# Attention's weighing products in blocks of two pieces, and the sign matrices copied to scratch in the read stage instead of stored by attention

## The reference, cut to what matters

```python
x = x + tanh(g_xattn) * layer(layernorm(x), pos, ...)     # layer: read, attention, write, read, mlp, write
x = x + tanh(g_ffn) * (layernorm(x) @ sign) * softplus(scale)

def attention(qkv_in, qkv_w, pos):        # 2 batches, 16 heads of 32, 1024 positions, causal
    q, k, v = projections; q, k = rope(q, pos), rope(k, pos)
    scores = where(tril, q k^T / sqrt(32), -1e30)
    p = softmax(scores); return p v
```

## Time and profile before

| | |
|---|---|
| median of 3 runs (range) | 2181.62 us (2178.24 to 2190.67) |
| profiled execution, its own time | 2191.2 us |
| its span, first to last instruction | 2189.2 us |
| read, attention and block stage in it | 365.3, 451.9 and 1372.0 us |
| busy in the span: PE, DVE, ACT, POOL | 90%, 61%, 40%, 22% |
| moved by transfers | 464.72 MB, mean 212 GB/s |

### The profile page before, as it was taken

How to read it: one execution, slowest core, us unless ns; L and a number is a source line. 1 busy time by engine, 2 the same in 40 slices (tenths; PEclk the granted TensorE clock), 3 DMA queues, 4 the chain that set the end, 5 groups by cost and what they waited for, 6 DMA issues and landing times.

```text
span 2189.2 us, 25299 instructions
## 1 busy us (share of the span) xinstructions
PE 1968.7 (90%) x9818; PEld 1345.7 (61%) x9818; DVE 1327.3 (61%) x1403; ACT 881.2 (40%) x1191; POOL 478.8 (22%) x362
## 2 busy tenths in 40 slices
PE   4789988999999994399989999999999999989997
PEld 0344456555555552178677777777777677666776
DVE  5476667546666638858468549558458567567100
ACT  4646653546666654162362430162530261432000
POOL 0022342786665630000000001000001100011010
PEclk8889997879999996699999999999999999999999
DMA  7548358999999814337467658677658677668676
GB/s 261 158 111 226 116 152 190 310 275 265 288 278 278 243 64 172 151 135 293 145 270 273 230 163 236 201 264 281 226 151 232 192 284 276 242 156 238 158 175 132
DMA packets 156283, 464.72 MB, mean 212 GB/s; under 512 B 34176, under 2 KB 34816, under 8 KB 138752
## 3 DMA queue, kind: packets, MB, share of 16 engines
q1 hardware_dynamic: 123568, 324.16, 47.6%
q0 software_dynamic: 30432, 128.46, 19.1%
q10 hardware_dynamic: 2160, 10.43, 1.3%
HBM read 323.79 MB, written 139.20 MB: 211 GB/s over the span
## 4 chain that ended last, share of the span: by engine, by line
PE 42%; DVE 7%; DMA 7%; ACT 4%; issue 2%; SPq 0%; POOL 0%; DVEq 0%; POOLq 0%; ACTq 0%
PE ps L1833 15%; PE ps L1643 8%; PE ps L1645 7%; PE ps L1644 7%; DMA sign_h<-sign_h_scratch 5%; DMA up<-up_s_scratch 2%; PE ps L1702 1%; PE ps L1711 1%; ACT L1862 1%; DVE Y L2156 1%; PE ps L1663 1%; PE ps L1752 1%; PE ps L1740 1%; DVE DL_attn L2063 0%; DVE E_attn L2068 0%
## 5 line engine op out<-in xcount | busy, mean ns | idle before, releaser
L1833 PE MATMUL ps<-XH,sign_h 128*128 128x512 f32 x768 | 310.2, 404 | 18.5 <-DMA sign_h<-sign_h_scratch 14.1
L1833 PE MATMUL ps<-XL,sign_h 128*128 128x512 f32 x768 | 303.6, 395 | 0.0
L1209 DVE TENSOR_REDUCE maxes<-ps 128x1 f32<-128x512 f32 (+3 forms) x384 | 208.0, 555 | 156.1 <-PE ps L1059 117.6
L1155 ACT ACTIVATE probs<-ps 128x512 f32<-128x512 f32 (+3 forms) x384 | 169.0, 489 | 133.5 <-PE ps L1086 86.5
L1643 PE MATMUL ps<-ZH,up 128*128 128x512 f32 x512 | 204.4, 399 | 13.6 <-DVE ZL L2181 8.9
L1645 PE MATMUL ps<-ZH,up 128*128 128x512 f32 x512 | 200.5, 392 | 0.0
L1644 PE MATMUL ps<-ZL,up 128*128 128x512 f32 x512 | 200.3, 391 | 0.0
L1833 PEld LDWEIGHTS ps<-XH,sign_h 128*128 128x128 f32 x768 | 146.6, 191 | 67.8 <-DMA sign_h<-sign_h_scratch 18.1
L1101 PE MATMUL ps<-probs,values 128*32 128x512 f32 (+3 forms) x768 | 170.0, 519 | 0.1
L1101 PE MATMUL ps<-probs,ones_sum 128*32 128x512 f32 (+3 forms) x768 | 170.0, 519 | 0.0
L1833 PEld LDWEIGHTS ps<-XL,sign_h 128*128 128x128 f32 x768 | 146.7, 191 | 31.9 <-issue 1.9
(11 more groups left out here) (337 smaller groups left out, 4156.5 us busy)
## 6 DMA issues: line engine op xcount, KB each, us to landing
sign_h<-sign_h_scratch SPq DMA_DIRECT2D x256, 256.0 KB, 4.3
up<-up_s_scratch SPq DMA_DIRECT2D x58, 1024.0 KB, 6.3
proj<-proj_s_scratch SPq DMA_DIRECT2D x58, 640.0 KB, 4.0
X<-in_x_read POOLq DMA_DIRECT2D x16, 1024.0 KB, 9.0
xn_scratch<-X SPq DMA_DIRECT2D x16, 1024.0 KB, 14.1
sign_raw<-in_sign SPq DMA_DIRECT2D x32, 512.0 KB, 10.2
sign_h_scratch<-sign_high SPq DMA_DIRECT2D x32, 512.0 KB, 8.1
up_s_scratch<-weight_split SPq DMA_DIRECT2D x16, 1024.0 KB, 8.7
```

Of the source, the lines that this page charges most:

```text
L1155: eng.activation(PT[p % NPT][:, e, 0:w], ps[:, score_bank(v, p, e), 0:w], ACT.Exp, scale=HD ** -0.5).then_inc(ex.sem, ex.unit)
L1209: eng.tensor_reduce(MAXES[:, e, q, k0 // T:k0 // T + 1], ps[:, ring_bank(n, ("max", m)), 0:w], AX.X, ALU.max).then_inc(mx_read.sem, mx_rea ...
L1833: mm = eng.matmul(ps[:, sign_bank(m)], s[q][:, f], x[:, n], start=n + w == 0, stop=n == NF - 1 and w == len(operands) - 1, skip_group_chec ...
```

## The change

Three edits.

1. `weigh` runs in blocks of two pieces. Round n handles its pieces in six groups of two: all scores and maxima of the two pieces, then `rows` if due, then the weighing of the two pieces before. The last two pieces of a pair are weighed at the start of the next round. In a piece, each of the two scores is now followed by its part of the maxima. There is a fourth buffer of probabilities.
2. Attention no longer stores the high halves of the signs. POOL still computes both halves, for the test whether a low half is needed.
3. The scratch that the last stage loads is filled by 16 transfers of 1 MB from the input tensor straight to the scratch tensor, in SP's queue of the read stage, four in each of the passes n = 1..4. (In the branch with low halves, the last stage would cut the signs itself.)

```diff
 read_phase, SP
+                def copy_sign(m):
+                    eng.dma_start(io["sign_s"][m], io["sign"][m]).then_inc(t["sign_copied"].sem, t["sign_copied"].unit)
                 for n in range(NB + 1):
+                    if n:
+                        copy_sign(4 * n - 4)
                     for tt in range(TT if n else 0):
                         store_v(n - 1, tt)
...
+                    if n:
+                        copy_sign(4 * n - 3)
                     for s in (1, 2):
                         for u in range(TT if n else 0):
                             store_qk(n - 1, s, u)
+                        if n:
+                            copy_sign(4 * n - 3 + s)
                     if 0 < n < NB:
                         load_turns(n)
 attention_phase
-        NPT = 3
+        NPT = 4
 SP
                 def store_weights(e, n):
-                    eng.wait_ge(probed.sem, probed.at(n, 2 * e + 2))
-                    eng.dma_start(io["sign_h"][n:n + 1, :, e * HF:(e + 1) * HF].rearrange("a p f o -> (a p) f o"), SIGN_H[e][:].bitcast(F32)
-                                  ).then_inc(sign_out[e].sem, sign_out[e].unit)
                     eng.wait_ge(weight_cut.sem, weight_cut.at(n, 2 * e + 2))
 POOL, probe
-                    past(eng, sign_out[e], n - 1)
 PE
+                def weigh_two(v, g):
+                    for p in (2 * g, 2 * g + 1):
+                        weigh(v, p)
                 for n in range(PAIRS + 1):
                     m = 0
-                    for p in range(NSC):
-                        if front(n - 1):
+                    if front(n - 2):
+                        weigh_two(n - 2, LAST_TWO)
+                    for g in range(NSC // 2):
+                        for p in (2 * g, 2 * g + 1):
                             for e in range(2):
-                                score(n - 1, p, e)
-                        for part in range(2):
-                            if part:
-                                if p and front(n - 1):
-                                    weigh(n - 1, p - 1)
-                                elif p == 0 and front(n - 2):
-                                    weigh(n - 2, NSC - 1)
-                            for _ in range(MAX_AT[p][part] if front(n) else 0):
-                                maxima(n, m)
-                                m += 1
...
+                                if front(n - 1):
+                                    score(n - 1, p, e)
+                                for _ in range(MAX_AT[p][e] if front(n) else 0):
+                                    maxima(n, m)
+                                    m += 1
...
+                        for p in (2 * g, 2 * g + 1):
+                            if p in ROW_AT and front(n):
+                                rows(n, ROW_AT[p])
+                        if g and front(n - 1):
+                            weigh_two(n - 1, g - 1)
```

34 lines of the change are left out of this document (20 added, 14 removed).

## The result

The changed kernel takes 2192.64 us in the median of 20 runs (2185.52 to 2200.99), the kernel before 2186.49 beside it (median of 20, from 2178.24; one of them took 2301.29); the ratio is 1.0031, with a 95% interval of 1.0019 to 1.0043. So it is slower, by 6.8 us by the ratio, a change smaller than the 0.5% used for the chances, where 2175 was forecast: 17.6 us too low, and 1.6 us above the forecast's range of 2156 to 2191. The profiled execution has a span of 2190.7 us.

The account below looks back on a forecast made before the run. The prediction took PE's pace to bound attention. Terms of -12.5 (rounds), -2 (stores), +7 (copies) and +1 (early rounds) sum to -6.5, set against the median 2181.62: forecast 2175 us, range 2156 to 2191.

Parts of the forecast that it names:

- A wait that comes: Attention rounds: PE's eighth score waits for ACT's exponential of score 5, 1.2 us of new wait per round.
- Rival 3: Copies cost more and late operands bring another stretch at 1.2 GHz: read stage +12, early rounds +10, 2191; chance 0.18.
- Blocks of two, the price of a switch: Attention rounds: seven switches into and out of weighing go, 0.23 us each, saving 1.6 us per round.
- a wait that goes: Attention rounds: PE's weight loads for weighings find their exponentials done, saving 0.3 us per round.
- The signs' copies: Read stage: 16 transfers of 1 MB at 3.4 us each, with little cover in three places; +7 in the read stage.
- (a): Read stage, fourth load of x: two copies in SP's queue against 1.6 us of cover make PE wait, +4 us.
- (b): Read stage's end: a turned q waits for a store of its buffer, delayed by the copy ahead, +3 us.
- (c): Start of attention: the sixteenth copy stands ahead of the first loads and delays POOL's first signs, +3.4 us.
- The stores that go: Attention: 32 sign stores of 512 KB leave; -2 us before late operands, +1 beyond the read stage's shift in early rounds.
- Rival 2: Attention's two early rounds: without the stores operands are in time and the clock stays 1.00, giving 2160; chance 0.16.
- Rival 1: Attention rounds: the new wait for ACT is absent and transfers stay hidden, rounds 23.0 us, total 2158; chance 0.15.
- Rival 4: Attention rounds: switching inside a block of weighings costs 0.23 each as outside, rounds +0.9, total 2195; chance 0.05.

Follow-up runs that it names:

- e6: The changed kernel with the reciprocal of the pair before moved one step later on ACT, behind the exponentials of scores 5 and 6; 2173.03 us, ratio 0.9932.
- e11: e6 with the second judging activation moved earlier on ACT, behind the exponentials of scores 3 and 4; 2188.25 us, ratio 1.0012.
- e16: The changed kernel with e11's edit, so both judgings and the reciprocal stand ahead of the exponential of score 5; 2222.37 us, ratio 1.0149.
- e8: The changed kernel with both the block of four weighings split and the reciprocal later on ACT; 2174.90 us, ratio 0.9947.
- e12: e6 with only the last four copies of the signs moved from the read stage into attention (rounds 5 to 8); 2164.26 us, ratio 0.9911.
- e1: The kernel before with only the blocks of two and the fourth probs buffer; sign stores kept, no copies; 2188.47 us, ratio 1.0008.
- e4: The changed kernel with a round's last block of weighings moved from the round's start to behind the first four scores; 2182.31 us, ratio 0.9960.
- e5: e1 with e4's edit, so sign stores stay in attention and no copies run; 2176.83 us, ratio 0.9951.
- e10: e1 with e6's edit, so sign stores stay in attention and no copies run; 2166.46 us, ratio 0.9913.
- e2: The kernel before with only the signs' copies added and their stores removed, weighing piece by piece as before; 2192.88 us, ratio 1.0022.
- e17: The kernel before, unaltered, run again for the profile of another execution; 2189.67 us.
- e18: e1, unaltered, run again for the profile of another execution; 2197.17 us.
- e3: The changed kernel with 1 of its 16 copies, the block stage loading that one piece sixteen times; 2194.86 us, ratio 1.0027.
- e7: e4 with the 16 copies issued in attention from the fifth round on instead of in the read stage; 2175.95 us, ratio 0.9944.
- e9: e6 with the 16 copies issued in attention from the fifth round on; 2167.12 us, ratio 0.9911.

## Why the prediction was wrong

Forecast and measurement by place, from the table, the mean of the two profiles of each kernel:

| place | forecast | measured |
|---|---|---|
| start of round 1 (read stage, first operands) | +7 | +9.0 |
| rounds 1 to 4 | -1.9 | -7.7 |
| rounds 5 to 15 | -9.9 | +2.1 |
| rest | -1.5 | +0.1 |
| sum | -6.3 | +3.5 |

(The sum of the forecast is -6.5 where its roundings are kept.) The runs' ratio says +6.8 (4.2 to 9.4). The 3 us between it and the two profiles are within what the rest varies by from one execution to the next. Against the forecast of 2175 the miss is larger, 17.6, since 4.9 of it lie in the base: the forecast starts from 2181.62, the median of three runs, and twenty give 2186.49.

Two rows of the table need a word. In the new order `rows` stand ahead of three weighings (pieces 2, 3 and 4) that stood ahead of them before. So round 1 as cut here has three weighings fewer and the rest three more: 19 pieces before and 22 after, worth 0.57 + 0.36 + 1.00 = 1.9 us at the full clock. Round 1 runs mostly at 1.2 GHz (clock 0.50 before, 0.56 after), so there they are worth up to twice that. By this estimate 2 to 4 of the 7.7 us that rounds 1 to 4 are shorter are work that moved out of them, and not a gain.

**The step that failed is the term "A wait that comes": "1.2 us of a new wait per round".** Its place, its releaser and nearly its size were right: 1.56 us from score to score where e6, without the wait, has 0.51, so 1.05. What it leaves out is what PE's clock does behind it: the term for that was nothing, without a reason given. Of 22 steady rounds in two profiles nine are 1.6 us longer, since PE runs the products behind the wait at 1.2 GHz: 0.65 per round, 7 us in eleven rounds. That this follows the wait is shown by four kernels that have the same PE order and differ in ACT's alone (and in one step of DVE's). With the wait at 0 it is gone (e6), with 0.67 it does not come (e11), with 1.05 it comes in four or five of eleven rounds, with 2.1 in all (e16). Why 1.05 brings it in one round and not in the next stays open. The price of the wait in the round is thus 0, 0.77, 1.15 to 2.75, and 3.8 us. The Trainium skill, TensorE: Matmul & The Clock Gate, A second HAM failure mode: psum-queue depth-cycling, has a kernel whose frequent small idles between groups of matmuls make the clock oscillate. The rounds here agree, with clocks of 0.94 and 1.00 in turn. Rival 3 had another stretch at 1.2 GHz in it, but from late operands; the prediction knew the fallen clock of the earlier trace rows and did not ask whether its own new wait could bring it. The trace of before had such a case: in the round of 35.4 us PE waits 1.57 us, and the products behind that wait run at 1.2 GHz (the row is below, under the stores). That is the lesson of the case.

**Blocks of two, the price of a switch.** 1.6 us a round was right, and so was zero from weighing to weighing. e6 has no wait left and is 1.60 shorter than before, which is 7 x 0.23. The one switch that e8 has more costs 0.15, so not each is worth the same. The Trainium skill, TensorEngine Tiling (Array Packing), Key Properties, says that a change of the tiling mode drains TensorE. By the two drains alone the prediction had 1.3, and the measured 1.60 is above that. The forecast had 2.1 without the new wait, so the 0.2 for masks and loads that pair better and the 0.3 for "a wait that goes" did not come on top. For the second the rows show why: PE was busy 25.02 of 25.10 us before, so the loads of the earlier trace rows that wait for `probs` lie under matmuls. Those 0.5 a round are 5.5 us in eleven rounds, the second part of the miss: 7 + 5.5, less 0.5 since the wait costs 1.15 and not 1.2, is the 12.0 of the table.

**The signs' copies.** +7 forecast, +9.0 measured, all of it in the read stage: attention's first instruction is 7.9 and 10.0 us later in the two profiles. (a) PE's wait for x is 3.46 (+4 forecast), and 2.8 in e6 and 2.7 in e12. The trace also tells which of the two copies counted: both. The first line is how long the four loads of x took to land, where the earlier trace rows has 7.4/12.9/17.1; the largest belongs to the last of them. The other lines are what SP's queue (q1) and POOL's (q0) moved from 196 to 199 us: packets, MB, share of the engines.
```profile
DMA to landing us min/median/max: 11.2/16.7/22.7
q1 hardware_dynamic: 43, 1.07, 84.8%
q0 software_dynamic: 31, 0.22, 21.6%
```
SP issued its second copy at 184.9, 5 us behind the last load of x, and still it passes between 196 and 199 us, while that load, which lands at 202.5, moves little. So x on POOL's queue does not keep its place, as the second reading of the prediction has it. The last load of x takes 16.9 to 17.3 us in the nine profiles without such copies and 21.7 to 22.7 in the eleven with them: 5 us for two copies, not 6.8. The stall is smaller than 5.2 for that reason, and because PE itself comes 0.85 later.

(b) The end costs 5 to 7 instead of 3. DVE waits 5.13 for a store, not 0.92, and e12, with the last four copies moved, does not have it. (c) POOL's first signs arrive 8.8 later, which is the shift of the stage, and its wait is only 0.8 longer.

Over ten profiles with all copies in the read stage round 1 starts at 380.9 in the mean, over nine with none or one there at 372.6. In the medians the copies' price is smaller: 1.0031 against 1.0008 (changed, e1), 0.9960 against 0.9951 (e4, e5), 0.9932 against 0.9913 (e6, e10), 2 to 5 us, each pair with overlapping intervals. That they cost something is seen in all three and in e2, whose interval lies above 1. How much stays open between 2 and 9.

**The stores that go.** -2 + 1 forecast, and the bound set for the two early rounds, 5 us, was passed: 66.7 before, 59.7 after. The wait for operands grew from 3.02 to 6.00, as forecast ("these rounds keep their length and the wait of 3.02 grows"), but the second long round is gone. That one had a wait of its own, for the next pair's operands, which the prediction does not name:
```profile
475.33 0.33 PE L1056 MATMUL ps<-turned_k,turned_q 96*128 96x128 f32 x1 [1.57 <-DMA turned_k<-qk_scratch]
```
In e17 it is 2.89. With it the clock falls in both. The changed kernel, e1 and e2 have no such wait in that round. Rival 2 put this down to the stores. e2, with the stores gone and the weighings as before, bears it out: its rounds are 29.7, 25.4, 31.6 and 25.1. But e1 keeps the stores and does not have the second wait either (23.4, 27.5, 36.2 and 24.6): its first one is 6.87, so PE is later and the next operands have landed. Both have 112 us in rounds 1 to 4, as both edits together. That the longer first wait covers the second in e1 is a reading that no run tests.

**The last round.** -1.5 forecast, and +0.1 in the table's rest, a part that varies by 13 us. The stretch from the first `rows` of round 16 to the last weighing repeats better: 45.2 us in both profiles of before, 45.6 in both of the changed kernel, with three weighings (1.9 us) more in it. So it saves 1.5, as forecast.

**The rivals.** Rival 1 (no new wait, 2158) is what e6 and e10 are, apart from the copies: its 23.0 us round is 23.5. Rival 4 is refuted by 0.43 from piece to piece. (Its sum was off too: 0.9 in 12 rounds and +6 for the transfers give 2198, not 2195.) Rival 3 gave the time, 2191, for other reasons: its read stage and its early rounds were both too dear. Its 2191 is near the measured time by luck. The chance of a result within 0.5%, 0.45, was the one that came.

## What to carry to other kernels

When a reordering removes work between two dependent engines, follow the other engine's chain at that place, and price the new wait twice: once as it is, and once with the matmul clock falling behind it, in some or all of the repetitions. Then look in the other engine's queue for what can stand one step later: here two activations moved by one step turned 1.0031 into 0.9932, a kernel slower than before into a faster one. Judge a change of 0.3% by the medians of many runs, and its mechanism by a part of the profile that repeats, such as the rounds here, not by the span of one profile.

## What the runs showed of the hardware

- A wait of PE of 0.67 us in each round of 24 us left the clock at 1.00 in all 33 rounds seen; 1.05 us brought 1.2 GHz in 9 of 22 (and in 13 of 33 of e1, e18 and e3), from one round to the next with the same instructions; 2.1 us in 11 of 11. In each case the stretch at 1.2 GHz begins behind the wait, 0.3 to 1.0 us after the start of the score that waited, and costs 1.6 us.
- Sixteen copies of 1 MB inside HBM, one or two in a round, do not lengthen a steady round (e7: 24.00 as e4; e9: 23.50 as e6), at a DMA share of 0.99:
```profile
578.70:602.20 23.50, 23.48 (x193) 15.05 (x194) 14.68 (x31) 16.25 (x35) 15.51 (x9) 1.00 0.99 280
```
- Two 1 MB copies on SP's queue delay the last of four 1 MB loads on POOL's queue by 5 us (17.2 to 22.2 us from issue to landing), although one of the copies is issued 5 us after that load.
- Seven switches fewer between matmuls of 128 and of 32 output partitions take 1.60 us off a round (e6 against before), one more adds 0.15 (e8 against e6).
- The same program's last 1420 us take up to 13 us more in one execution than in another, at an unchanged order of instructions.
